# The causal mask of the first attention's maxima: added on the vector engine and not on TensorE

## The reference

```
q, k = concat(rmsnorm parts, rotary-like parts)       # per head
scores = einsum('bhqd,bhkd->bhqk', q, k) * scale
causal = triu(full((t, t), -inf), k=1)
attn = softmax(scores + causal, axis=-1)
ctx = einsum('bhqk,bhkd->bhqd', attn, v_c)
x = x + einsum('bhtd,od->bhto', ctx, W_O)
```

## Time and profile before

| | us |
|---|---|
| runs: 1568.40, 1558.43, 1567.13; median | 1567.13 |
| profiled execution, whole | 1563.78 |
| its span, first to last instruction | 1561.3 |
| TensorE busy | 1306.3 (84%) |
| DVE busy | 1012.3 (65%) |
| ACT busy | 844.6 (54%) |
| POOL busy | 565.9 (36%) |
| first and last start of L1008 | 72.4 and 377.0 |

### The profile page before, as it was taken

How to read it: one execution, slowest core, us unless ns; L and a number is a source line. 1 busy time by engine, 2 the same in 40 slices (tenths; PEclk the granted TensorE clock), 3 DMA queues, 4 the chain that set the end, 5 groups by cost and what they waited for, 6 DMA issues and landing times. The chain is left out here.

```text
span 1561.3 us, 40898 instructions
## 1 busy us (share of the span) xinstructions
PE 1306.3 (84%) x12473; PEld 817.1 (52%) x12535; DVE 1012.3 (65%) x3815; ACT 844.6 (54%) x1629; POOL 565.9 (36%) x808
## 2 busy tenths in 40 slices
PE   2399999997699999996896599999999543999998
PEld 1155555554466666664673366666666332555555
DVE  2267777774366666664553488787787725887774
ACT  1167777775377777775222467666677332223221
POOL 3457777772122222220100155555554521121120
PEclk9999999999599999999898599999999665999999
DMA  5000000000000000000000477677677321000000
GB/s 156 1 1 2 0 0 0 0 2 1 1 2 2 0 0 0 0 1 1 1 0 0 111 203 203 186 206 201 177 210 203 85 65 44 8 8 14 8 7 14
DMA packets 152050, 82.90 MB, mean 53 GB/s; under 512 B 6874, under 2 KB 150372, under 8 KB 151828
## 3 DMA queue, kind: packets, MB, share of 16 engines
q1 hardware_dynamic: 151428, 79.65, 18.7%
q0 software_dynamic: 528, 2.10, 0.5%
HBM read 43.72 MB, written 38.01 MB: 52 GB/s over the span
## 5 line engine op out<-in xcount | busy, mean ns | idle before, releaser
L761 POOL TENSOR_TENSOR rr<-ms_eps,minus_half 128x16 f32<-128x16 f32 x64 | 184.8, 2905 | 92.6 <-DVE ms_eps L969 92.6
L1090 DVE TENSOR_REDUCE rowmax<-psum 128x4 f32<-128x768 f32 x128 | 122.1, 954 | 71.6 <-PE psum L1986 71.4
L1268 DVE CUSTOM_DVE_ANT_0 summed<-psum,pos_score 128x128 f32<-128x128 f32 x512 | 117.9, 286 | 52.9 <-PE psum L2195 42.5
L504 PE MATMUL psum<-identb,stacks 128*128 128x128 bf16 x1544 | 126.9, 229 | 28.0 <-DVE stacks L497 22.5
L1008 DVE TENSOR_REDUCE rowmax<-psum 128x4 f32<-128x512 f32 x128 | 88.2, 689 | 61.1 <-PE psum L1862 59.9
L504 PEld LDWEIGHTS psum<-identb,stacks 128*128 128x128 bf16 x1544 | 95.6, 102 | 61.0 <-DVE stacks L497 29.8
L1807 ACT ACTIVATE pos_rows<-psum 128x512 f32<-128x512 f32 x72 | 43.0, 597 | 152.5 <-PE psum L2318 151.9
L595 PE MATMUL psum<-probsT,values 128*32 128x128 f32 x2048 | 111.3, 290 | 1.7 <-DVE attn L621 1.2
L1698 ACT ACTIVATE pos_rows<-psum 128x512 f32<-128x512 f32 x128 | 76.9, 601 | 59.6 <-PE psum L2186 57.2
L1704 ACT ACTIVATE probsT<-psum 128x512 f32<-128x512 f32 x128 | 76.5, 598 | 39.4 <-PE psum L2207 39.3
L369 POOL TENSOR_TENSOR rstd<-vareps,minus_half 128x4 f32 (+1 forms) x24 | 24.4, 1016 | 202.0 <-DVE vareps L360 202.0
(11 more groups left out here) (258 smaller groups left out, 3196.5 us busy)
## 6 DMA issues: line engine op xcount, KB each, us to landing
skew<-pos_rows SPq DMA_DIRECT2D x128, 258.0 KB, 4.6
pos_score<-skew SPq DMA_DIRECT2D x128, 256.0 KB, 4.2
X<-in_x_dram POOLq DMA_DIRECT2D x1, 2048.0 KB, 12.2
ctxT<-in_ctx_dram SPq DMA_DIRECT2D x1, 2048.0 KB, 10.5
y_rows<-hidden SPq DMA_DIRECT2D x8, 256.0 KB, 2.4
yT<-y_rows SPq DMA_DIRECT2D x4, 512.0 KB, 5.4
out_dram<-X SPq DMA_DIRECT2D x8, 256.0 KB, 2.3
w_up<-in_L_ffn_w_e_dram SPq DMA_DIRECT2D x2, 512.0 KB, 4.1
```

Source lines behind the costliest of these rows:

```text
L504: last = pe.transpose(turned[:, t, :], stacks[:, which, 2 * t:2 * t + 2, :].rearrange("s h k -> s (h k)"), identb[:, :])
L761: pool.tensor_tensor(out=rr[:, par, i * H:(i + 1) * H], in0=ms_eps[:, i * H:(i + 1) * H], in1=minus_half[:, 0:H], op=ALU.pow).then_inc(A.r ...
L1090: dve.tensor_reduce(rowmax[:, par, first:first + 2 * PT - 1:2].rearrange("s (b h) -> s b h", b=2), B.max_space, AX.X, ALU.max, negate=True ...
L1268: last = dve.tensor_tensor_reduce(summed[:, r % 2, p, :], P.score_bank[r % 2][:, p, :], pos_score[:, par, r * PT + p, :], 1.0, -3.0e38, AL ...
```

## The change

In `largest`, the one reduction over 512 columns is replaced by four operations over 128 columns, each adding the float32 mask from `consts` to one head's scores, negating the sum and taking the minimum of it into `rowmax`. The sums themselves are written to `summed`, a buffer of a later stage. A semaphore increment stands ahead of them. In `score`, the matmul of identity and mask is left out, and the four score matmuls write and do not accumulate. The second pass keeps its mask product.

```diff
@@ def largest(n, par, r)  [DVE]
                 wait(dve, A.s, n * R + r + 1)
                 if r == 0:
                     wait(dve, A.nm, 2 * (n - 1))
-                first = head(r, 0)
-                dve.tensor_reduce(rowmax[:, par, first:first + 2 * PT - 1:2], A.max_bank[r % 2].rearrange("s (p k) -> s p k", p=PT),
-                                  AX.X, ALU.max, negate=True).then_inc(A.mx, 1)
+                dve.sem_inc(k0.carry, 1)
+                for p in range(PT):
+                    h = head(r, p)
+                    last = dve.tensor_tensor_reduce(summed[:, r % 2, p, :], A.max_bank[r % 2][:, p * S:(p + 1) * S],
+                                                    consts[:, C_CAUSAL:C_CAUSAL + S], -1.0, 3.0e38, ALU.add, ALU.min,
+                                                    rowmax[:, par, h:h + 1])
+                last.then_inc(A.mx, 1)
@@ def score(n, par, four, r)  [TensorE]
                 wait(pe, A.mx, n * R + r - 1)
                 to = A.max_bank[r % 2]
-                pe.matmul(to, identb[:, :], causal4[:, :, :].rearrange("s p k -> s (p k)"),
-                          start=True, stop=False, skip_group_check=True)
                 for p in range(PT):
                     last = pe.matmul(to[:, p * S:(p + 1) * S], rows_of(qT[:, par, :, :], r, p),
-                                     rows_of(keysT[:, four, :, :], r, p), start=False, stop=(p == PT - 1),
-                                     skip_group_check=True)
+                                     rows_of(keysT[:, four, :, :], r, p), start=True, stop=True)
                 last.then_inc(A.s, 1)
```

## The result

The changed kernel's median is 1588.9 us against 1567.4 for the kernel before on the same chip; the ratio is 1.0164, with a 95% interval of 1.0116 to 1.0212. That is +21.5 us where the forecast was +7, inside the range given and above the limit of 1583 for "no change".

What follows compares the result with a forecast made beforehand. TensorE, at 9.57 us a body, bounded the kernel before; a ring through DVE would bound it after, at 10.00. +11.2 - 2.2 - 0.5 - 1.2 = +7.3 us gave 1574 us; range 1556 to 1600, own range 1564 to 1582.

Steps and rivals of the forecast that it cites:

- the ring: Dependent chain through DVE, TensorE and ACT in a first-attention body: 9.32 us before the change, 10.00 us after.
- TensorE's sum: TensorE's own work in a first-attention body: falls from 9.57 to 8.29 us without four mask products of 0.32 us.
- the four groups: DVE's four operations for each r: r = 0, 1, 2 cost 0.24 us more each, r = 3 0.22.
- bodies 1 to 26: First-attention bodies carrying all the work: +0.43 us each, +11.2 us together.
- bodies 27 to 30: First-attention bodies without layer norm on DVE: TensorE's gain comes through in part, -0.3 us each, -1.2 together.
- paying whole durations: Rival: each of DVE's four operations pays its whole duration; +32 us, 1599 us, chance 0.05.
- the late starts: DVE groups after a wait begin 0.20 us later; 0.10 us taken in all where DVE is busy ahead, behind L969.
- No DMA, no ACT work, no other order changes: Claim that DMA, ACT work and other order stay the same, and SP and POOL queues carry what they did.
- Nothing: Cost claimed for the carry semaphore's increment, the write of the sum into `summed` and the read of the mask.
- Late starts in every group: Rival: each of DVE's four groups in a body pays 0.20 us; +20 us, 1587 us, chance 0.17.
- The clock: Rival: idle TensorE falls to 1.2 GHz in the first attention; five falls +14 us, 1589 us, chance 0.15.
- DVE fills its waits: Rival: only DVE's own time counts in a first-attention body, 8.8 to 8.85 us; -23 us, 1544 us, chance 0.10.

Runs made afterwards that it cites:

- without the loop: DVE's first-attention loop over quads written out, so that it takes no branch there: changed kernel 1557.8 us (0.9958), kernel before 1556.9 us (0.9931).
- the shifted one: Changed kernel with its DVE loop kept and 39 semaphore increments added at the very start of DVE's stream: 1575.4 us, ratio 1.0057.
- the move of `rms_sum`: DVE's loop written out, sums of squares taken after the placing of the maxima: changed kernel 1548.3 us (0.9887), kernel before 1556.3 us (0.9946).
- TensorE's part alone: Kernel before, DVE's loop written out, first pass's mask product left out and one maximum kept, so maxima ignore the causal mask: 1524.2 us, ratio 0.9737.

## Why the forecast was right on the ring, and 15 us short

The ring, its size without the loop and its releasers are as forecast. That the range held is luck: 1588.9 lies outside the forecast's own 1564 to 1582, the rivals that widened the range (1587, 1589, 1599) did not happen as they were described, and what did, a stop behind DVE's branches, was in none of them. One of the prediction's own signs of being wrong came true, a granted clock below 1.00 in this stage (0.91).

**TensorE's sum, the four groups and the bound.** Right. Starts inside a group lie 0.21 apart, group to next operation 0.85 (forecast 0.84 to 0.85), last group to placing 0.97 (forecast 0.73 + 0.22 = 0.95). L1896 is released by L1022 and L1873 by ACT, as forecast. The rule of the Trainium skill that the prediction weighed ("VectorE: DVE Perf Modes", "Rules for kernel authors"), by which each chained operation waits for the one before to drain, is not borne out: starts 0.21 us apart at a duration of 0.29. Without the loop the ring is 9.95 us against the 10.00 forecast, and the stage is +5.9 us against +7.3: bodies 1 to 26 +9.6 (forecast +11.2), body 0 -2.0 (-2.2), the first scores -0.4 (-0.5), bodies 27 to 30 -1.3 (36.3 to 35.0; forecast -1.2). Two small slips of the prediction: paying whole durations would cost 1.16 - 0.84 = 0.32 more in three of the groups, not 0.23 (the sum hardly changes), and the custom operation's late start was called constant from one row.

**Inside the loop the ring is 10.22.** Mis-sized by 0.22 us: the late starts. Against the same body written out, start to start: L966 to L969 0.55 instead of 0.45, L969 to L1010 0.27 instead of 0.16 (before: 0.11; I took +0.10, it is +0.16), and 0.05 more each behind L1000 and the second L497. The kernel before has the first of these too (0.54 in its loop, 0.44 written out), under TensorE's cover. Why operations start later in a loop isn't shown. In the loop without stops the body is 10.23 against 9.97: 20 bodies times 0.26 are 5.2 us, and the four branches another 1.1. Against that its first two bodies are 2.9 us shorter than the written-out kernel's (10.2 and 10.0 against 11.4 and 11.8; the granted clock reaches 1.00 at 85 us there and at 95 in the written-out kernel), and its last four are 1.2 longer. Together the stage is 4.6 longer.

**"No DMA, no ACT work, no other order changes" and "Nothing" for the increment.** This is the step that failed. I priced instructions where they run, and not the stream that they make. The loop went from 221 to 345 instructions, and at its place in the queue each taken branch costs DVE 2.6 us more (2.93 on the mean against 0.3), and "no DMA" was wrong in just this: instructions are fetched by DMA. Sum of the changed kernel against the shifted one: four long bodies of 13.3 instead of 10.5, +11.1; four slow ones behind them, 1.0 + 0.7 + 0.7 + 0.6 = +3.0; together 14.1 of the 14.9 measured in the stage. The chain is: branch, no instructions for DVE for 3 us, TensorE idle, clock down to 0.50, a slow body.

So of +25.4 us in the stage: +5.9 the change itself, +4.6 the loop without stops (slower starts and branches +6.3, the last four bodies +1.2, the clock's rise in the first two -2.9), +14.9 the stops. With the 4.8 us that the rest of the program ran shorter, the two profiled executions are some 20 us apart; the medians are 21.5 apart, and no run here was made to explain the rest of the program.

**The rivals.** Late starts in every group: no, behind work they are 0.05 to 0.16. The clock: my rival had it fall five times from TensorE's idle share alone. At that share, in the written-out kernel, it stays at 1.00 through the stage; in the shifted one it falls once. In the changed kernel it falls seven times, four of them 2 to 5 us behind the end of a stop and three (229, 274, 318 us) midway between stops; that those three follow from the stops is likely and not shown. The rule that the prediction took from the Trainium skill ("TensorE: Matmul & The Clock Gate", "HAM oscillation — how this bites in real kernels"), that a TensorE which idles between groups can be set back to half its clock, agrees with the falls behind a stop. Read as a rule on the idle share, as the rival did, it was too gloomy: an idle share of a fifth alone left the clock at 1.00. DVE fills its waits: not by itself, but the move of `rms_sum` did just that.

**What is shown of the stop, and what is open.** Shown: it follows a taken branch, needs no change of content to go away (39 instructions ahead suffice), and comes with 24 more instruction packets. Loops here, by the place of their first instruction in DVE's queue and their length, both counted in the trace:

| place | length | gap behind the branch, us |
|---|---|---|
| 261 (before) | 221 | 0.33 to 0.38 |
| 342 | 281 | 0.30 to 0.36 |
| 422 (changed) | 345 | 2.78 to 3.02 |
| 461 | 345 | 0.28 to 0.33 |
| 461 | 349 | 0.28 to 0.33 |
| 552 | 345 | 2.78 to 3.05 |
| experts' loop: 2230, 2470, 2726, 2856 | 282 | 2.84, 3.67, 3.68, 3.41 |
| experts' loop: 2556, 2765, 2826, 3308, 3722, 3820 | 282 | 0.30 to 0.34 |

Shorter loops, of 8 to 221 instructions, never stop in any of the kernels: 340 taken branches, at most 0.38 us.

The kept traces say more, though no run was made for it. In the changed kernel with its loop written out, a packet of the instruction queue, 8192 bytes, starts when DVE's queue has come to its 578th, 705th, 836th, 963rd, 1095th, 1222nd and 1349th instruction (142 to 249 us): one for every 128, 65 to 71 behind a multiple of 128. After the taken branches of the changed kernel's loop the first packet starts 1.0 to 1.2 us later, and in that time the written-out queue goes on by 7 to 9 instructions (128 in 17.8 us). So I estimate that the queue comes in blocks of 128, with borders 56 to 64 behind a multiple of 128. With any border in just this span, the six loops of the table that stop (the experts' loops counted one by one) touch four blocks, and the ten that don't touch three. By these sixteen, a taken branch goes on at once here when three blocks hold the whole loop. This was read out of the traces afterwards; a kernel shifted to a place that it names would test it.

The Trainium skill, "Runtime: NRT & Kernel Launch", section "Instruction fetch mechanics", says that instructions come in blocks of 256, that two blocks are held, and that a branch taken to a target outside them stalls for a fetch. The trace agrees that a taken branch can stall, that where it lies decides, and that packets are fetched for it. It doesn't agree on the size. With blocks of 256 counted from the first instruction of the trace the rule would have 461 to 806 stall (it touches three blocks) and 422 to 767 not (two), and it is the other way round; counted from any other origin it is right in at most 14 of the sixteen.

## What to carry to other kernels

Before a change adds instructions to a loop, ask two things beside their durations: whose ring they lengthen when the full engine is relieved, and where the loop's taken branch will land; a gap of 3 us behind a branch that the profile pins on some semaphore is to be checked against the queue's own branch and next instruction. Writing the loop out is the safe form here. And once the bound has moved, look for work to move out of the new ring: that gave back 13.1 us of the stage, twice what the change costs without the loop (6.1), and made the change a gain. With both, the changed kernel takes 1548.3 us, 0.9887 of the kernel before, the lowest here that keeps the causal mask (the version without the increment, at 0.9898, can't be told from it). The two together were not run.

## What was unexpected

- A semaphore increment on DVE has a duration of 21 ns and costs 0.09 us (200 of them 18.3 us, 130 of them 11.8), and 0.2 us when it stands between a wait and the operation behind it (score to first operation 0.62 us with it, 0.43 without).
- A stop behind a taken branch of 2.8 to 3.7 us on DVE, on and off by 39 instructions of shift. The kernel before has one itself, 2.84 us in the experts' loop.
- Writing out one loop of DVE makes the kernel before 0.7% faster, though the stage of that loop is no shorter. Most of this is unexplained.
- With TensorE's part alone a body is 8.78 us, where the ring as read gives 9.32 - 0.32 = 9.00. Half of the difference is the loop, which that kernel doesn't have: L966 to the maximum of r = 3 takes 0.53 us there and 0.65 in the kernel before. The other half is open. A ring read in bodies that another engine paces is an upper bound, so was this one.
